# A graph layer on one core: more rows gathered from the queues of SyncE and ScalarE, node tiles ordered singly, t stored in halves

## What is computed

```python
h = maximum(layernorm(x, axis=-1), 0)
agg = segment_sum(h[src], dst, 12500)
z = (1 + eps_gin) * h + agg
t = relu(batchnorm(z @ W1 + b1, g1, bt1))        # 12500 x 512
out = relu(batchnorm(t @ W2 + b2 + h, g2, bt2))  # 12500 x 256
return x + out
```

## Time and profile before

| | |
|---|---|
| median of 3 executions | 2143.56 us (2143.31 to 2145.06) |
| the profiled execution, its own time | 2143.43 us |
| its span, first to last instruction | 2141.6 us |
| PE / PE weight loads, busy | 1430.6 / 911.2 us |
| DVE / ScalarE, busy | 768.3 / 338.3 us |
| POOL, busy | 1449.2 us |
| mean granted TensorE clock | 0.831 of full speed |
| DMA queue of POOL | 200.64 MB, 32.0% of the 16 engines' span |
| DMA queue of SyncE (q1) / ScalarE (q10) | 97.34 MB, 12.8% / 25.75 MB, 3.6% |

### The profile page before, as it was taken

One profiled execution on the slowest core, in us unless ns is written; L12 is line 12 of the kernel. 1 busy time (PEld: TensorE's weight loads), 2 busy tenths in 40 slices (PEclk: granted clock), 3 DMA queues, 4 the chain that ended last, 5 costly groups with the idle time before them and its releaser, 6 DMA issues.

```text
span 2141.6 us, 24025 instructions
## 1 busy us (share of the span) xinstructions
PE 1430.6 (67%) x4835; PEld 911.2 (43%) x4835; DVE 768.3 (36%) x1947; ACT 338.3 (16%) x661; POOL 1449.2 (68%) x1540
## 2 busy tenths in 40 slices
PE   3656666665655766675666566666666666689998
PEld 2434344443433434343444334434344444454446
DVE  7777753222322222322232222222232232234447
ACT  6767660000000000000000000000000000014446
POOL 7777777777777777777777777777777777760000
PEclk7788788877888787888888887778787788899999
DMA  6666654444434434444444443443443444448438
GB/s 200 214 224 218 225 175 129 132 117 139 138 108 139 138 110 136 137 118 130 136 126 119 138 139 108 138 137 107 140 137 108 136 135 123 137 133 321 176 135 319
DMA packets 123554, 325.22 MB, mean 152 GB/s; under 512 B 32179, under 2 KB 55294, under 8 KB 117266
## 3 DMA queue, kind: packets, MB, share of 16 engines
q0 software_dynamic: 73440, 200.64, 32.0%
q1 hardware_dynamic: 39100, 97.34, 12.8%
q10 hardware_dynamic: 10870, 25.75, 3.6%
HBM read 271.55 MB, written 52.05 MB: 151 GB/s over the span
## 4 chain that ended last, share of the span: by engine, by line
POOL 65%; issue 21%; PE 12%; DMA 2%; ACT 0%; DVE 0%; SPq 0%; POOLq 0%; DVEq 0%
POOL arena L650 65%; PE ps L1442 8%; PE ps L1324 2%; PE ps L1456 2%; DMA arena<-h_rows,arena 1%; PE ps L1360 0%; PE ps L1398 0%; DMA arena<-in_src 0%; ACT aggT L1072 0%; SPq L439 0%; ACT arena L1078 0%; ACT arena L1076 0%; DVE arena L1057 0%; PE ps L1334 0%; SPq L433 0%
## 5 line engine op out<-in xcount | busy, mean ns | idle before, releaser
L650 POOL DMA_INDIRECT arena<-h_rows,arena x1292 | 1221.6, 946 | 394.0 <-issue 391.5
L1324 PE MATMUL ps<-arena 128*96 128x256 f32 x3060 | 976.9, 489 | 675.2 <-DMA arena<-h_rows,arena 561.5
L1324 PEld LDWEIGHTS ps<-arena 128*96 128x96 f32 x3060 | 640.8, 216 | 993.3 <-issue 732.4
L840 DVE TENSOR_TENSOR aggT<-aggT,ps 128x192 f32 x196 | 69.3, 353 | 1074.2 <-PE ps L1334 1071.2
L1151 ACT COPY arena<-ps 96x256 f32<-96x256 f32 x37 | 13.2, 357 | 1575.5 <-PE ps L1334 1545.0
L650 POOL DMA_INDIRECT arena<-in_x,arena x222 | 209.9, 946 | 67.7 <-issue 67.7
L1360 PE MATMUL ps<-arena 128*128 128x512 f32 (+3 forms) x412 | 186.3, 577 | 1.6 <-DVE arena L873 1.5
L1442 PE MATMUL ps<-arena,W2s 128*128 128x512 f32 (+1 forms) x400 | 168.1, 582 | 0.9 <-ACT arena L1272 0.8
L927 DVE TENSOR_TENSOR arena<-arena,ps 128x768 f32<-128x768 f32 x159 | 149.8, 942 | 0.0
L1103 ACT ACTIVATE arena<-arena,nb,mv 128x256 f32<-128x256 f32 x238 | 120.2, 587 | 83.6 <-DVE nb L744 81.5
L1442 PEld LDWEIGHTS ps<-arena,W2s 128*128 128x128 f32 x400 | 75.7, 190 | 93.2 <-issue 86.3
(11 more groups left out here) (99 smaller groups left out, 575.2 us busy)
## 6 DMA issues: line engine op xcount, KB each, us to landing
W2s<-h_rows ACTq DMA_DIRECT2D x2176, 1.0 KB
rl_odd<-h_rows SPq DMA_DIRECT2D x1792, 1.0 KB
t_T<-arena SPq DMA_DIRECT2D x24, 1024.0 KB, 4.9
arena<-t_T SPq DMA_DIRECT2D x24, 1024.0 KB, 4.8
arena<-h_rows,arena POOLq DMA_INDIRECT x1292, 2.8
arena<-in_x SPq DMA_DIRECT2D x27, 512.0 KB, 5.7
h_rows<-arena ACTq DMA_DIRECT2D x24, 512.0 KB, 3.4
out<-arena SPq DMA_DIRECT2D x23, 512.0 KB
```

Of the source, the lines that this page charges most:

```text
L650: nc.gpsimd.indirect_dma_start(out=rows[slot(g)][:, k, :], out_offset=None, in_=(x if g < H_FROM else h_dram)[:, :], in_offset=bass.Indire ...
L840: V.tensor_tensor(z, z, winT_ps, ALU.add).then_inc(s_add, 1)
L1324: last = T.matmul(win_ps[g % 2], sel[:, g % 2, k, :], rows_of(g, k), start=k == 0, stop=k == n - 1)
```

## The change

`SP_EIGHTHS` goes from 12 to 22 (44 rows a pass for 24) and `ACT_EIGHTHS` from 7 to 11 (22 rows a group for 14). Node tiles of the second stage are loaded singly, three passes ahead, into eight buffers in the same place in SBUF, each with a semaphore of its own; a load waits for the transpose of the tile eight before it. The chunks of t but the last two are stored in two halves of two blocks (512 KB), the first half in pass 4n, as soon as its two blocks are there, the second in pass 4n + 1; the waits on `s_td` count 32 for a chunk in place of 16.

```diff
-SP_EIGHTHS = 12
-ACT_EIGHTHS = 7
+SP_EIGHTHS = 22
+ACT_EIGHTHS = 11
+HALF_T = FB // 2
-QUAD = 4
+NODE_BUFS = 8
+NODES_AHEAD = 4
...
+        node_rows = ring[:, 2 * GT * D:3 * GT * D].rearrange("p (j d) -> p j d", d=D)
...
+        def node_tile(c):
+
+            return node_rows[:, (c - H_NODES) % NODE_BUFS, :]
+
+        def node_count(c):
+
+            return 16 * ((c - H_NODES) // NODE_BUFS + 1)
...
-            def load_quad(k):
-                if k >= 2:
-                    sp.wait_ge(s_hT, H_NODES + QUAD * (k - 1))
-                first = H_NODES + QUAD * k
-                n = QUAD if k < NQUAD - 1 else QUAD - 1
-                sp.dma_start(quads[k % 2][:, 0:n, :],
...
+            def load_node_rows(c):
+                n = P if c < NT - 1 else LASTN
+                if c - NODE_BUFS >= H_NODES:
+                    sp.wait_ge(s_hT, c - NODE_BUFS + 1)
+                sp.dma_start(node_tile(c)[0:n, :], h_dram[c * P:c * P + n, :]
+                             ).then_inc(s_node[(c - H_NODES) % NODE_BUFS], 16)
+
+            def store_half_t(q, half):
+                a, b = half * HALF_T, (half + 1) * HALF_T
+                sp.wait_ge(s_tb, FB * q + b)
+                sp.dma_start(t_dram[q, :, a:b, :], tb[:, a:b, :]).then_inc(s_td, 16)
...
                 if c == NT - 1:
-                    store_t(NQF - 2)
+                    for half in (0, 1):
+                        store_half_t(NQF - 2, half)
                 if c < H_NODES:
                     load_node_tile(c)
                 elif c == H_NODES:
                     wait_h(sp)
-                    load_quad(0)
-                    load_quad(1)
-                elif (c - H_NODES) % QUAD == 2 and (c - H_NODES) // QUAD + 2 < NQUAD + 1:
-                    k = (c - H_NODES) // QUAD + 1
-                    if k >= 2:
-                        load_quad(k)
-                if 2 * Q < c < NT - 1 and c % Q == 1:
-                    q = (c - 2 * Q - 1) // Q
-                    if q == NQF - 3:
-                        sp.wait_ge(s_td, 16 * q)
+                    for n in range(NODES_AHEAD):
+                        load_node_rows(c + n)
+                elif c + NODES_AHEAD - 1 < NT:
+                    load_node_rows(c + NODES_AHEAD - 1)
+                if 2 * Q <= c < NT - 1 and c % Q <= 1:
+                    q, half = divmod(c - 2 * Q, Q)
+                    if q == NQF - 3 and half == 0:
+                        sp.wait_ge(s_td, 32 * q)
                         load_t(0, 0, 0)
-                    store_t(q)
+                    if q <= NQF - 3:
+                        store_half_t(q, half)
...
-            sp.wait_ge(s_td, 16 * (NQF - 1))
+            sp.wait_ge(s_td, 32 * (NQF - 1))
...
-                        dve.wait_ge(s_td, 16 * q)
+                        dve.wait_ge(s_td, 32 * q)
...
-                    k = (c - H_NODES) // QUAD
-                    pe.wait_ge(s_quad[k % 2], quad_count(k))
-                h = hx if c < H_NODES else quad_tile(c)
+                    pe.wait_ge(s_node[(c - H_NODES) % NODE_BUFS], node_count(c))
+                h = hx if c < H_NODES else node_tile(c)
```

More of the change, by code:

```diff
@@ L152, in build @@
               (ring[:, 2 * GT * D:3 * GT * D], work[:, 2 * GT * D:3 * GT * D]) for n in (0, 1)]
-        quads = [ring[:, 2 * GT * D + n * QUAD * D:2 * GT * D + (n + 1) * QUAD * D].rearrange("p (j d) -> p j d", d=D)
-                 for n in (0, 1)]
-        assert (NT - H_NODES) % QUAD == 0 and 2 * QUAD == GT
+        node_rows = ring[:, 2 * GT * D:3 * GT * D].rearrange("p (j d) -> p j d", d=D)
+        assert NODE_BUFS == GT
         after_rows = [work[:, 3 * GT * D + n * D:3 * GT * D + (n + 1) * D] for n in range(4)]
@@ L272, in build @@
         s_xt = [sem("s_xt_even"), sem("s_xt_odd")]
-        s_quad = [sem("s_quad_even"), sem("s_quad_odd")]
+        s_node = [sem(f"s_node{b}") for b in range(NODE_BUFS)]
         s_ev, s_wT = sem("s_ev"), sem("s_wT")
@@ L475, in store_t @@
                 if q < NQF:
-                    sp.dma_start(t_dram[q, :, :, :], tb[:, :, :]).then_inc(s_td if q < NQF - 1 else s_td_full, 16)
+                    sp.dma_start(t_dram[q, :, :, :], tb[:, :, :]).then_inc(s_td_full, 16)
                 else:
@@ L1156, in t_and_b1 @@
                     if m == 0:
-                        act.wait_ge(s_td, 16 * q)
+                        act.wait_ge(s_td, 32 * q)
                     act.wait_ge(s_tst, FB * (q - 1) + m + 1)
```

## The result

The changed kernel takes **2161.1 us** (median of 4, 2159.0 to 2163.8) against 2143.4 (2143.0 to 2145.1): the ratio is 1.0082, with a 95% interval of 1.0064 to 1.0099. It is slower by 18 us, where 30 us less were predicted, and outside the range of 2110 to 2127. Its profiled execution took 2159.01 us, with a span of 2157.2.

The account below looks back on a forecast made before the run. It took POOL's gathers, 1.25 us each, to bound the kernel until 1917 us, with an unchanged part after. Profiled 2143.43 - 31.3 for 25 fewer gathers + 1 for the hand-over = 2113 us, range 2110 to 2127.

Parts of the forecast that it names:

- POOL's count: Until 1917 us, time is the number of POOL's gathers times 1.25 us; 25 fewer gathers save 31.3 us.
- (b): ScalarE's row queue: a tile each 5.82 groups, 54.5 us of work in 55.7 us, fits with 2% over.
- First stage: Groups below 30: SyncE's 44 rows a pass take 20 us, passes 19.6 apart; PE's slack for group 26 is 5.4 us.
- hand-over: Groups 29 to 33: ScalarE's rows delay window copies by 13 us, 7 us stay; nothing to some 5 us, taken as 1.
- end: After the last gathers: later W2 load and shorter last half store cost 0, bounds -1 to +1 us.
- (f): The hand-over, groups 29 to 33: more ScalarE row pieces ahead of window copies, taken as 1 us of stall.
- (c): SyncE's queue: a cycle of four passes takes 75.3 us against POOL's 76.6; 44 us of lateness covered, 78.9 a cycle bearable.
- (d): Second stage's single node tiles and half stores: worth nothing by themselves, cost nothing unless SyncE is late.
- A row of the DMA engines: Single rows, if all through one engine: 80 ns a row, engine 81% busy after the change, no backlog.
- rival 3: The engine carrying the rows fills up, deciding at 122 ns a row; at 130 ns 60 us, 2173 us; chance 0.05.
- Rival 2: SyncE bound by table loads of 4.2 us: cycle 82.3, 2180 us; chance 0.03 slower, 0.03 with part of the gain.

Follow-up runs that it names:

- 31 + 22 tiles: The changed kernel with ACT_EIGHTHS 9 in place of 11 (31 tiles for SyncE, 22 for ScalarE): 2118.2 us, ratio 0.9873 to the kernel before.
- 31 + 17 tiles: The changed kernel with ACT_EIGHTHS 7 in place of 11 (31 tiles for SyncE, 17 for ScalarE): 2124.9 us, ratio 0.9906 to the kernel before.

## Why the prediction was wrong

**What held.** 1.25 us a gather, 25 fewer, 31.3 us, and that nothing but POOL's count sets the time as long as nobody else is late: four other settings of shares came within 1 us of it. ScalarE keeps up ((b); 51.5 to 53.2 us a tile between 526 and 963 us), though its rows' packets start 10.7 us after their issue (median, 700 to 800), where they started after 1.1. First stage, hand-over and end cost nothing that shows: 31 + 22 tiles are on POOL's count without the 1 us of (f). SyncE's cycle of 75.3 us in (c) was right while the engine behind it was free: 75.9 and 74.5 at first, 74.7 at the end. The table loads behind a half store took up to 3.9 us. (d) was right about the node tiles and the half stores. (The 630.7 us that SyncE waited before were 19 waits, not 20; nothing hangs on it.)

**The step that failed** is "A row of the DMA engines": the 80 ns a row, and the 81% of one engine that it gave. It was taken from 30 us in which both queues worked, with the words that as many packets came by as were issued, so no backlog grew. In the earlier trace rows 79 rows were issued by SyncE and 146 packets passed, which is 73 rows: six had stayed behind in 30 us. About three are on their way at any time (ScalarE's packets start 1.1 us after the issue when nothing is behind); the rest was the beginning of a backlog, and ScalarE's rows, 1.1 us from issue to packet at 430 us, took 2 to 3 us by 460. At a load that never stops the row costs 113 ns on the mean of both queues: 352 x 0.113 / 82.2 = 48% for the rows, 36% for the gathers and some 6% for t and node tiles, 90%. The prediction's condition for rival 3, that the sum reaches 100% at 122 ns a row, failed as well: the rows were late below it. And with POOL's packets halved they were late at 79%, while 31 + 17 tiles with 74% (700 to 1600 us) and 31 + 22 with 81% (1500 to 1600 us) have no backlog. These sums are estimates from the single packets and the DMA views. So the sum of the packets' times doesn't by itself say when the engine is full.

Rival 3 is what came; it was given a chance of 0.05. That its price, 2173, is near the 2161 measured is partly luck: it rests on 130 ns and on a full engine of 100%, and it doesn't take off the 44 us of lateness covered in (c), with which it would be 2129. What holds is (c)'s own reckoning with the measured cycle: fifteen cycles of 82.2 us are 15 x 5.6 = 84 us over POOL's, less 44 is 40, and POOL's waits cost 46.9.

**The way it went on** is (c)'s: SyncE's queue lengthens, its issues slow down, the cycle is 82.2 us on the mean, and POOL's first wait over 0.3 us comes between 900 and 1000 us. One half of it wasn't in the prediction: the stores of t stand in the same queue, so their last sixteenth sets out some 20 us after the issue, and DVE, which waits for them before it writes t again, waits 286 us in all. (d) had said "unless SyncE is late", and both were late: the last packets set out 12.5 to 23.2 us after the issue, and as DVE's longest wait, 29.8 us, is longer than that, in that case the issue came late as well. Rival 2 (slow table loads) didn't come: their median is 2.13 us as before.

The Trainium skill's rule (DMA: Bandwidth & Descriptors, on why a DMA increments its semaphore by 16) that a hardware-queued copy on few engines takes the lowest-numbered ones was the right warning, and the late sixteenth of the stores agrees with it as far as it goes: one engine for both queues, of which number no view tells. On arbitration the same page (Queues, rings and completion order) says that an engine drains a whole packet of one queue's ring before it turns to the next. The trace agrees: away from node tile loads 87% of neighbouring rows are of different queues in the changed kernel and 46% in the one before. As a row is a packet here and its semaphore another, a row takes two turns.

## What to carry to other kernels

DMAs of one row each cost their issuing queue little (0.32 us), and all of them met in one DMA engine here, whichever queue issued them. Add up that engine's account (rows, semaphore writes, its share of the large transfers) as one resource, and price a row by a stretch in which the load is lasting, since a backlog of a few rows in a short burst is the first sign that it is full. Don't wait for the account to reach 100%: in this kernel 74 and 81% were borne, and 90%, and 79% of another make-up, were not. Below that limit a share moved off POOL was worth its full price, and 20 moved tiles gave 25 us; five more took 43. What another engine waits for, as the store of t, had better not stand in a queue behind such rows; a kernel with the store elsewhere was not run.

## What the runs showed of the hardware beyond that

- A large transfer behind a backlog of single rows lands as late as the rows (22 us for 128 KB that took 3.8), as one of its sixteen parts is in the crowded engine: 120 of a half store's 128 packets start within 3.8 us of the issue, the other eight not before 9.9 us, and 18 to 21 us behind it by the medians.
- A single-row DMA takes 46 ns for 1 KB (median) and 9 ns for its semaphore write, 75 ns on the mean in the kernel before and 113 ns on the mean of both queues where a backlog stands.
- The time of the same kernel was 2143 to 2145 us in some runs and 2573 to 2601 in others, with single moves and issues of SyncE held up to 1.4 us; the cause was not found.
